# Second attention of a four-layer block on one core: scores in four row groups, division after the weighing, and jobs that run on over batch borders

## The reference, cut to what matters

```
def _L1_attn_ref(x, Wq, Wk, Wv, Wo, rel_emb):        # 16 heads of 8 channels, 256 tokens
    q = heads_split(x @ Wq); k = heads_split(x @ Wk); v = heads_split(x @ Wv)
    q = q * cos + _rotate_half(q) * sin
    k = k * cos + _rotate_half(k) * sin
    bias = rel_emb[buckets].transpose(2, 0, 1)[None]
    scores = jnp.einsum('bhqd,bhkd->bhqk', q, k) / sqrt(HD) + bias
    scores = jnp.where(causal, scores, jnp.float32(-1000000000.0))
    attn = jax.nn.softmax(scores, axis=-1)
    ctx = jnp.einsum('bhqk,bhkd->bhqd', attn, v)
    ctx = ctx.transpose(0, 2, 1, 3).reshape(b, s, d)
    return ctx @ Wo
```

## Time and profile before

| what | value |
|---|---|
| median of 3 runs | 2419.14 us (2418.79 to 2419.44) |
| the profiled execution's own time | 2419.39 us |
| its span, first to last instruction | 2417.5 us |
| busy, share of the span | PE 94%, PEld 65%, DVE 73%, ACT 57%, POOL 66% |
| mean granted TensorE clock | 0.974 of full speed |

### The profile page before, as it was taken

The page is one execution under the profiler, slowest core; times in us unless marked ns, Lnnn a source line. Parts: engine busy times, 40 slices in busy tenths (PEclk is TensorE's granted clock), DMA queues, the critical chain, the costliest instruction groups (busy, mean ns, idle before and its releaser), DMA issues.

```text
span 2417.5 us, 81630 instructions
## 1 busy us (share of the span) xinstructions
PE 2280.3 (94%) x34944; PEld 1563.9 (65%) x34944; DVE 1755.6 (73%) x2707; ACT 1379.3 (57%) x2778; POOL 1596.8 (66%) x931
## 2 busy tenths in 40 slices
PE   7789999999999999999999999999968888889998
PEld 5456666666666666666666666666646666656665
DVE  3678887888788878887888788878838888822322
ACT  2256666666666666666666666666626666633332
POOL 1298888898889888988898889888912322101111
PEclk9899999999999999999999999999979999989999
DMA  4011112111221112111221112211130000000000
GB/s 115 3 38 36 33 35 66 44 34 33 57 53 34 34 31 70 42 34 32 54 58 34 31 36 60 52 32 35 35 113 1 1 1 1 1 1 5 5 5 5
DMA packets 77303, 83.91 MB, mean 35 GB/s; under 512 B 24964, under 2 KB 48786, under 8 KB 76946
## 3 DMA queue, kind: packets, MB, share of 16 engines
q1 hardware_dynamic: 76946, 78.70, 12.7%
HBM read 26.56 MB, written 1.07 MB: 11 GB/s over the span
## 4 chain that ended last, share of the span: by engine, by line
PE 62%; DVE 20%; issue 10%; ACT 5%; POOL 3%; SPq 0%; ACTq 0%; DMA 0%; POOLq 0%; DVEq 0%
PE bank L564 8%; PE bank L645 7%; PE bank L657 6%; DVE n L1266 5%; PE lnbank L585 4%; PE obank L634 4%; ACT qk L941 3%; PE bank L575 3%; PE obank L626 3%; PE sbank L601 3%; PE bank L665 3%; PE bank L856 3%; PE obank L611 3%; PE obank L866 2%; PE sbank L866 2%
## 5 line engine op out<-in xcount | busy, mean ns | idle before, releaser
L1259 DVE TENSOR_TENSOR qk<-bank,tab 128x1024 f32<-128x1024 f32 x384 | 468.7, 1221 | 194.7 <-ACT qk L941 194.6
L1577 POOL TENSOR_TENSOR rn<-n2m,cst 128x16 f32<-128x16 f32 x192 | 562.8, 2931 | 16.0
L1573 POOL TENSOR_TENSOR qk<-qk 128x1024 f32<-128x1024 f32 x192 | 454.6, 2368 | 156.9 <-DVE qk L1259 156.9
L564 PE MATMUL bank<-wqk,xs 128*128 128x512 f32 x768 | 405.0, 609 | 1.7 <-DVE qk L1259 0.9
L941 ACT ACTIVATE qk<-bank 128x512 f32<-128x512 f32 x384 | 226.9, 591 | 314.0 <-PE bank L564 314.0
L1581 POOL TENSOR_TENSOR qk<-qk,rn 128x1024 f32<-128x1024 f32 x192 | 365.4, 1903 | 28.1 <-POOL rn L1577 0.9
L575 PEld LDWEIGHTS bank<-cst,qk 128*128 128x128 f32 x1536 | 191.5, 141 | 215.3 <-issue 170.7
L575 PE MATMUL bank<-cst,qk 128*128 128x128 f32 x1536 | 231.8, 274 | 11.0 <-POOL qk L1581 11.0
L1266 DVE TENSOR_REDUCE n<-qk 128x16 f32<-128x1024 f32 x192 | 232.1, 1209 | 0.0
L1585 POOL TENSOR_TENSOR lnr<-lnv,cst 128x2 f32<-128x2 f32 (+1 forms) x76 | 54.3, 714 | 244.1 <-DVE lnv L1143 244.1
L585 PE MATMUL lnbank<-wv,xs 128*64 128x512 f32 x768 | 208.0, 620 | 0.0
(11 more groups left out here) (357 smaller groups left out, 4231.0 us busy)
## 6 DMA issues: line engine op xcount, KB each, us to landing
vp<-vp SPq DMA_DIRECT2D x672, 65.0 KB, 2.0
wqk<-in_L_ffn_Wqkv SPq DMA_DIRECT2D x24, 256.0 KB, 3.6
wv<-in_L_ffn_Wqkv SPq DMA_DIRECT2D x6, 512.0 KB, 3.9
wo<-in_L_ffn_Wo SPq DMA_DIRECT2D x6, 512.0 KB, 4.2
xs<-Z SPq DMA_DIRECT2D x48, 64.0 KB, 2.4
xs<-Z SPq DMA_DIRECT2D x48, 63.8 KB, 2.1
vp<-in_L_ffn_w SPq DMA_DIRECT2D x1, 2048.0 KB, 13.7
mw<-in_L_ffn_w SPq DMA_DIRECT2D x8, 256.0 KB, 6.8
```

Of the source, the lines that this page charges most:

```text
L564: nc.tensor.matmul(bank[s % 2][:, :], xs[:, odd, WIN + r * P:WIN + r * P + P], wqk[:, lo:lo + 512], start=True, stop=True).then_inc(p_full, 1)
L1259: tt(qk[:, both, :].rearrange("p o (h d) -> p o h d", d=DH), heads(bank[c % 2][:, :]).unsqueeze(1).broadcast_to([P, 2, PAIRS, DH]), table. ...
L1573: tt(direct, direct, swapped, ALU.add).then_inc(sum_done, 1)
L1577: tt(rn[:, m % 2, :], n2m[:, :], const("mhalf"), ALU.pow).then_inc(rn_done, 1)
```

## The change

The scores of a block (all three jobs) are made together. `quad` joins the four banks that were `sbank` and `obank`. Head h = 4g + y lies in row group g (partitions 32g to 32g+31), so the four heads of one y are multiplied in four row groups of 32 rows, each into its own bank. Half 0 takes columns 0 to 127 of each bank and half 1 columns 128 to 383. There is one set of banks now: the scores of the next block wait for the maximum of the last job of this one. They stand at the end of slots 2, 5, 8, and, for the next batch, 11.

The multiplication of `px` by the reciprocals goes. ACT copies the weighed values undivided (`take_raw`), PE spreads the reciprocals over the partitions with 16 small matmuls for each half of a batch (`spread_inverses`), and DVE multiplies once for each half (`divide3`). There is one reciprocal instruction for each half instead of one for each job.

Slots run on: a batch has 12 slots, and the transposes and weighings of its last jobs stand in the first slots of the next batch. `px` and `sh` get a third buffer (`ao`). `finish` moves to slots 8 to 11. On ACT the order in a slot changes: `finish` and `prepare` first, then the exponentials of job m, then the copy of job m-2; before, the copy of job m-2 came first, then the exponentials, then `prepare` and `finish`. The layer norm's squares are part of `prepare` and `finish`.

`bias` gets a place of its own, and its transfer (2 MB) stands in the SP queue behind the first round of stage 2; the experts' `mw2` takes the place that it had. `mask_q` makes two instructions of 4 x 128 columns for each batch instead of four of 8 x 128. Adding the bias and taking the maximum stay two instructions.

```diff
-JOBS = [job for n in range(0, H, 4)
-        for job in ((0, range(n, n + 4)), (1, range(n, n + 2)), (1, range(n + 2, n + 4)))]
+JOBS = [job for y in range(4)
+        for job in ((0, range(y, H, 4)), (1, range(y, H // 2, 4)), (1, range(H // 2 + y, H, 4)))]
...
+            sp.dma_start(bias[:, :, :], bass.AP(relu_dram.ap().tensor, 0, [[1, P], [384, H], [1, S]])).then_inc(rel_in, 16)
...
+            def scores3(b, odd, y):
+                if y == 0:
+                    pe.wait_ge(s3["qk"], 2 * b + 2)
+                    pe.wait_ge(s3["qm"], b + 1)
+
+                wait(pe, s3["mx"], NJ * b + 3 * y)
+                for r in range(2):
                     w = P * (r + 1)
+                    for g in range(4):
+                        rows = slice(WIN * g, WIN * g + WIN)
+                        mm = nc.tensor.matmul(quad[:, g, P * r:P * r + w], qm[rows, odd, y, r * P:r * P + P],
+                                              s3k[odd][rows, 0:w], start=True, stop=True)
+                mm.then_inc(s3["full"], 1)
+
+            def turn3(n):
+
+                pe.wait_ge(s3["px"], n + 1)
+                wait(pe, s3["pts"], n)
+                for q in range(4):
+                    mm = nc.tensor.transpose(bank[2][:, q * P:q * P + P], s3px[n % 3][:, q * P:q * P + P], ident)
+                mm.then_inc(s3["ptf"], 1)
...
+            def spread_inverses(b, half):
+
+                pe.wait_ge(s3["rdn"], 2 * b + half + 1)
+                pe.wait_ge(s3["raw"], 2 * b + half + 1)
+                for y in range(2):
+                    for r in range(2):
+                        lo = y * S + r * P
+                        for g in range(4):
+                            mm = nc.tensor.matmul(bank[half][WIN * g:WIN * g + WIN, lo:lo + P],
+                                                  rdn[:, half, y, r, g:g + 1].broadcast_to([P, WIN]), ident, start=True, stop=True)
+                mm.then_inc(s3["rdw"], 1)
...
-                for m in range(NJ + 3):
-                    attend(b, odd, m)
+                for m in range(NJ if next_batch else NJ + 4):
+                    n = NJ * b + m
+                    if 2 <= n <= NJ * B + 1:
+                        turn3(n - 2)
+                    if 3 <= n <= NJ * B + 2:
+                        weigh3(n - 3)
                     if next_batch:
                         prepare(b + 1, m, u if batch_before else LN_S3 + 2)
                     if batch_before:
-                        finish(b - 1, m, u + 2 if next_batch else u, next_batch)
+                        finish(b - 1, m, u + 2 if next_batch else u)
+                    if m == 3 and batch_before:
+                        spread_inverses(b - 1, 1)
+                    if m == 9:
+                        spread_inverses(b, 0)
+                    if m == 15:
+                        spread_inverses(b, 1)
+                    if m in (2, 5, 8):
+                        scores3(b, odd, m // 3 + 1)
+                    if m == NJ - 1 and next_batch:
+                        scores3(b + 1, 1 - odd, 0)
...
-                for m in range(NJ + 3):
-                    attend(b, m)
+                for m in range(NJ if next_batch else NJ + 3):
+                    n = NJ * b + m
+                    if batch_before:
+                        finish(b - 1, m, u + 2 if next_batch else u)
                     if next_batch:
                         prepare(b + 1, 1 - odd, m, u if batch_before else LN_S3 + 2)
-                    if batch_before:
-                        finish(b - 1, m, u + 2 if next_batch else u)
-                    if m in (10, 14):
-                        take_out3(b, odd, m // 14)
+                    if m < NJ:
+                        exps3(b, m)
+                    if 2 <= n <= NJ * B + 1:
+                        take_turned3(n - 2)
+                    if m == 2 and batch_before:
+                        take_raw(b - 1, 1)
+                    if m in (8, 14):
+                        take_raw(b, m // 14)
...
-            def normalise3(b, m):
-                r, hs = JOBS[m]
-                n = len(hs)
-                dve.wait_ge(s3["px"], NJ * b + m + 1)
-                nc.vector.reciprocal(rdn[:, m % 2, 0:n], dn[:, m % 2, 0:n]).then_inc(s3["rdn"], 1)
-                dve.wait_ge(s3["rdn"], NJ * b + m + 1)
-                part = px[:, m % 2, :].rearrange("p (h n) -> p h n", h=n)
-                tt(part, part, rdn[:, m % 2, 0:n].unsqueeze(2).broadcast_to([P, n, P * (r + 1)]), ALU.mult).then_inc(s3["pn"], 1)
+            def divide3(b, half):
+
+                dve.wait_ge(s3["rdw"], 2 * b + half + 1)
+                wait(dve, s3["y"], b)
+                tt(aoTf[:, 512 * half:512 * half + 512].rearrange("p (c t) -> p c t", c=4),
+                   s3raw[half].rearrange("p (c t) -> p c t", c=4),
+                   bank[half][:, :].rearrange("p (c t) -> p c t", c=4)[:, :, ::-1], ALU.mult).then_inc(s3["ot"], 1)
```

More of the change, by code:

```diff
@@ L167, in build @@
         w1t = rotf[:, 512:1024]
-        mw2 = sb("mw2", [P, NE, 4, DIM])
+        bias = sb("bias", [P, H, S])
         sh = sb("sh", [P, 2, 512])
@@ L188, in build @@
         tabf = tab[:, :, :, :, :].rearrange("p l k r d -> p (l k r d)")
-        bias = [f[:, 0:PAIRS * S].rearrange("p (h t) -> p h t", h=PAIRS) for f in (kTf, tabf)]
+        mw2 = [f[:, 0:NE * EF // 2].rearrange("p (e c n) -> p e c n", e=NE // 2, c=4) for f in (kTf, tabf)]
         relv = sb("relv", [WIN, H])
@@ new lines, in turn3, with weigh3 @@
+            def turn3(n):
[4 more added lines that the diff above has]
+                mm.then_inc(s3["ptf"], 1)
+            def weigh3(n):
+                b, m = n // NJ, n % NJ
+                r, heads = JOBS[m]
+                y = m // 3
+                pe.wait_ge(s3["pts"], n + 1)
+                if m == 0:
+                    pe.wait_ge(s3["v"], b + 1)
+                if m in (0, 6):
+                    wait(pe, s3["ot"], 2 * b - 1 + m // 6)
+                lo = (y % 2) * S + r * P
+                for kb in range(r + 1):
+                    for x, h in enumerate(heads):
+                        row, q = WIN * (h // 4), x * (r + 1) + kb
+                        mm = nc.tensor.matmul(bank[y // 2][row:row + WIN, lo:lo + P], vs[:, b % 2, kb, h, :],
+                                              pT[:, n % 2, q * P:q * P + P], start=(kb == 0), stop=(kb == r))
+                mm.then_inc(s3["pv"], 1)
@@ L834, in _ @@
             step3(B - 1, 1, False, True)
-            for slot in range(9, 13):
-                finish(B - 1, slot, LN_S4 - 1, False)
+            for slot in range(8, 12):
+                finish(B - 1, slot, LN_S4 - 1)
             pe.wait_ge(ld_gate, 64)
@@ L1047, in finish @@
             def finish(b, slot, u):
+                if slot == 8:
+                    act.wait_ge(s3["y"], b + 1)
+                    nc.scalar.copy(s3y, lnbank[:, S:2 * S]).then_inc(s3["ys"], 1)
                 if slot == 9:
[L1049 to L1051 removed]
                     ln_sq_act(S, u)
[L1054 to L1069 removed]
@@ new lines, in exps3 @@
+            def exps3(b, m):
+                n = NJ * b + m
+                r, heads = JOBS[m]
+                w = P * (r + 1)
+                act.wait_ge(s3["mx"], n + 1)
+                wait(act, s3["ptf"], n - 2)
+                if m in (0, 6):
+                    wait(act, s3["rdn"], 2 * b - 1 + m // 6)
+                for x, h in enumerate(heads):
+                    g = h // 4
+                    last = nc.scalar.activation(s3px[n % 3][:, x * w:x * w + w], s3sh[n % 3][:, x * w:x * w + w], ACT.Exp,
+                                                bias=mx[:, n % 3, x:x + 1],
+                                                accum_out=dn[:, m // 6, (m // 3) % 2, r, g:g + 1])
+                last.then_inc(s3["px"], 1)
```

193 lines of the change are left out of this document (77 added, 116 removed).

## The result

| | median us | runs | ratio to before, 95% interval |
|---|---|---|---|
| before | 2418.97 | 4, 2417.86 to 2419.44 | |
| after | 2468.84 | 4, 2466.4 to 2470.83 | 1.021, 1.0197 to 1.0222 |

The change makes the kernel 2.1% slower, about 50 us. The forecast was 2450 us with a range from 2410 to 2488.

A forecast was written before the change was run, and what follows sets the result against it. The prediction took stage 3 to be bound by a ring of waits among PE, ACT and DVE, not by an engine's busy time. From 2419.4 us, +19 for the ring and +12 for the clock gave 2450 us, range 2410 to 2488.

The forecast's parts named there:

- The ring: Stage 3: engines waiting for each other in a circle set a batch's time, 41.4 us in the middle; +19 us.
- The six steps: Chain through a layer-norm block of stage 3, from one end of ACT's copy to another: 9.7 us.
- Step 1: Norm block, PE: handoff, transposes, weighing and mean after ACT's copy, done at 1.69 us.
- step 6: Norm block, ACT: third job's exponentials, then copy, done at 9.70 us; PE's next scores start beside it at 8.15.
- The low clock: PE's idle gaps in stage 3's norm blocks: 15 clock falls at 0.4 to 1.3 us each, +12 us (0 to +30).
- the rival in which every gap falls to the low level: Stage 3: every PE gap brings the low clock, 2468 us; chance 0.17 shared with serial scores.
- Spreading and dividing: Stage 3: 16 spreading matmuls and a multiplication per half batch are hidden; without cover 29 us in all.
- Scores in row groups: Stage 3, PE: a block's scores take 1.1 to 1.5 us, bounds 0.85 and 2.75; nothing in the sum.
- the rival in which the row groups take turns: Stage 3 scores run serially, above 1.6 us a block: 2478 us; chance 0.17 shared with the low-clock case.
- Bias in stage 2: The 2 MB bias transfer, now in stage 2, costs 0, or 9 us once if its cover is gone.
- The signs that were named: Stage 3: batches 40 to 43 us; ACT idle before squares and `out3`'s copy, DVE before epsilon; more low clock; scores 1.1 to 1.5.
- The rival in which the norm steps do not hold the ring: Stage 3: mean and variance come a slot earlier, batch 31 us, kernel 2358 us; chance 0.21 together with a mis-sized ring.

The follow-up runs named there:

- e8: Changed kernel plus eight small matmuls with unused results behind the norm's mean on PE in slots 0, 3 and 9; 2435.56 us.
- e1: Changed kernel with ACT's slot order put back: copy of job m-2, exponentials of job m, then the neighbouring batches' steps; 2348.04 us.
- e3: Changed kernel with ACT's slot order as before and PE's norm steps ahead of transposes and weighing; 2379.77 us.
- e6: Changed kernel with only ACT's copy of job m-2 moved ahead of the exponentials, squares still first; 2373.45 us.
- e7: Changed kernel with ACT's slot order as before and the division of each job's `px` back on DVE; 2383.35 us.
- e2: Changed kernel with PE's norm steps and projections ahead of transposes and weighing in a slot, ACT's order unchanged; 2406.63 us.
- e5: Changed kernel with only ACT's `finish` and `prepare` (squares) moved behind the exponentials, copy still last; 2439.54 us.
- e4: Changed kernel with the division of each job's `px` back on DVE, ACT's order as in the changed kernel; 2486.86 us.

## Why the prediction was right in its cause and short in one term

**The ring (predicted +19 us): right.** At full clock a middle batch takes 41.2 us (e8), predicted 41.4. Its blocks, from scores to scores in the batch from 1932.14, are 9.57, 9.74, 11.46 and 10.44, predicted 9.7, 9.7, 12.3 and 9.7. The last two differ because `out3` lets PE issue the fourth block's scores before ACT's copies are done; together they are 21.9, predicted 22.0. In stage 3 of e8 the first seven batches take 283.3 us against 272.7, and the last 51.1 against 43.2: +18.5, and less 0.8 by an earlier start +17.6 at the stage's end. That this is so near 19 is in part luck, since its terms missed both ways: the six middle batches gave +14.1 for +16 (246.6 us against 232.5), the first batch and the start -4.4 for -2, the last batch +7.9 for +5. The medians give +17.5 (2435.56 - 2418.08), but e8's runs lie in two pairs, 2431 to 2433 and 2438 to 2439 us, and its median between them, so they confirm the size only roughly. The earlier start is not the mask's doing as forecast: the changed kernel starts stage 3 when before does, and the starts of the eight kernels of the experiments scatter from 1810.8 to 1814.1.

The six steps can be laid beside the changed kernel's timeline, from the end of the copy at 1990.38. Step 1 ended at 2.36 instead of 1.69, and from there each step kept its size: the exponentials done at 4.71 (4.05), the variance at 7.15 (6.47), the last copy at 10.27 (9.70). The 0.6 or 0.7 is the scores of the block, which stood at 1989.93 ahead of the transposes and lasted 1.23 us. I had them beside step 6. They are hidden there at full clock, as e8's 9.57 shows, and come out when the transposes and weighing before them run at the lower clock.

**The low clock (predicted +12 us, 0 to +30): the term that was mis-sized.** The medians of the changed kernel and e8 differ by 33.3 us, of which 4.6 lie in stage 4 by the profiles; from the first scores to the end of stage 3 the two profiles differ by 28.3. Ring and clock, 18.5 + 28.3, are the 46.7 us by which stage 3 grew, where 19 + 12 = 31 were predicted. The step said 15 falls at 0.4 to 1.3 us each. Only the levels 0.50 and 1.00 occur, so a mean of 0.85 over 306.07 us and of 0.80 over 56.59 are 92 and 23 us at the lower level, 114 in all, against some 25 before (0.96 over 315.50). The changed kernel's clock fell 18 times from the first scores until just behind the stage. e8's fell 3 times, so there are the 15 falls of the prediction between them, and 28.3 / 15 = 1.9 us for each (the falls are counted in the trace's clock records). It is a mean with a wide scatter: the batch from 1989.93 has two falls and lies 0.7 us above 41.2, the one from 1897.89 has three and the rest of a fourth and lies 5.9 above. I had counted only transposes, weighing and variance behind a gap as slowed, 1.8 us of work; a fall lasted 3.4 to 10.2 us within the stage, long enough for the weighing of the next slot and the block's scores too. For the scores the timeline above shows it; how the 28.3 us divide among the slowed steps it does not show. The end of the stage shows slowed work in the open, in the last items of the changed kernel (`out3` took 1.97 before):

```profile
2165.38 1.94 PE L826 MATMUL bank<-cst,rdn 128*32 128x128 f32 x32 [0.78 <-ACT hT L1108]
2168.20 3.59 PE L744 MATMUL lnbank<-aoT,wv 128*128 128x256 f32 x8 [0.89 <-DVE aoT L1471]
```

The same spreading lasted 1.08 us where the clock was full. The measured 2468.84 us is to the microsecond the 2468 of the rival in which every gap falls to the low level, but not by that way: two of the three gaps of the batch from 1989.93 were followed by a fall, there were 18 falls in the stage and not one for each of 24 gaps, and on the mean they cost more than the 0.4 to 1.3 us that I took. The Trainium skill, "TensorE: Matmul & The Clock Gate", section "HAM oscillation — how this bites in real kernels", has a kernel that loses the clock at every wait between its bursts of matmuls, which there are waits for transfers. This trace agrees that such a kernel loses it again and again, and not that each of its gaps, of some 3 us, does it.

**Spreading and dividing: hidden, as predicted, by the timeline.** It stands behind the mean, in time in which PE would wait; e8's second block, which has it, takes 9.74 us and the first, which has not, 9.57, so that at most 0.2 us of it shows there. No run leaves it out alone. DVE's busy time is 23.7 us a batch, predicted 24 or 25. What the prediction did not say is that twelve multiplications would have stood in the ring: undone alone, the division costs 18 us more, and 35 with ACT's order of before.

**Scores in row groups: faster than I took them.** The eight matmuls of a block (16 instructions) last 0.94 us in all at full clock:

```profile
2021.37 0.94 PE L787 MATMUL quad<-qk 32*128 32x128 f32 x16
```

I took 1.1 to 1.5, with bounds of 0.85 and 2.75; the rival in which the row groups take turns fell. The Trainium skill's figure for four row tiles, by which I had estimated 0.83 (the same page, section "Part 3: Packing small matmuls — row/col tiling"), was nearer, as was my lower bound of 0.85.

**Bias in stage 2: nothing, as predicted.** Its 2 MB landed in 9.5 us, and stage 3 started at the same time as before, 1814.50.

```profile
bias<-rel_by_distance SPq DMA_DIRECT2D x1, 2048.0 KB, 9.5
```

**The signs that were named** came but for two. ACT was idle ahead of the squares three times a batch, released by the difference (6.9 us, at most 2.9); DVE was idle ahead of epsilon (6.6, at most 3.0); ACT waited 3.7 for `out3`; there was more of the lower clock. The scores were shorter than the 1.1 to 1.5 us named, and only one of the six middle batches, 41.9 us, lay in the 40 to 43 named; the others took 43.5 to 47.1, which is the clock. The rival in which the norm steps do not hold the ring (2358 us) is not what the changed kernel does, but it is nearly what e1 is: the mechanism was real, and one order of statements on ACT decides between the two.

## What to carry to other kernels

Where engines work in program order and hand each other work, write the slot of each engine down and follow the ring: an instruction that releases another engine's work (here the copy to `pT`) belongs ahead of the ones that wait for a third engine, and the same calls of a slot in another order were worth 121 us of 2469. Work taken off the fullest engine was worth less in the long ring (18 us) than in the short one (35). Price a new gap on TensorE with the clock: put a few matmuls of no use into the gap once, and what the kernel gains is what the gaps cost beyond their own length.

## What the runs showed of the hardware

- A low clock costs less than its length: some 95 us more at the lower level in the changed kernel's stage 3 than in e8's (114 against 2 x 0.02 x 283.31 + 2 x 0.07 x 51.10 = 18) went with 28.3 us of time, 0.3 us for each. At half the speed they could have cost half of the 95, an estimate for PE busy all through and always on the ring; what is missing to that fell into waits.
- With eight small matmuls in each of three gaps the clock stayed at 1.00 in all middle batches, although PE still waited 7.1 us a batch for the copy.
- Stage 4, which is the same code, took 287.3 us behind the changed kernel's stage 3 and 282.8 behind e8's. From 40 us into it on the rows of PE alone, of the changed kernel and of e8, are

```profile
2217.00:2464.50 247.50, 224.52 (x1235) 0.95 0.02 5
```

```profile
2188.00:2430.90 242.90, 219.87 (x1229) 0.97 0.02 5
```

so the 4.6 us lie in this part and come with a higher mean clock. What decides it I did not find; the profiles of before, e3, e6 and e7 have the longer one (286.9 to 287.5), those of e1, e2 and e5 the shorter (282.6 to 283.0), and e4's is between, 285.1. A difference of 5 us between two kernels of this family need not come from the stage that was changed.
